# Inverse roots moved to ScalarE and VectorE in the attention part, scatters without an address check in the expert part

## What is computed

```python
q = q / jnp.linalg.norm(q, axis=-1, keepdims=True)      # k too, per head of 32
A = jnp.einsum('bnihd,bnjhd->bnij', Kb, K)              # chunks of 64 tokens
T = inverse of (I + tril(A, -1)); W = T @ Kb; U = T @ Vb
u_i = u0 - w_i * Sd[:, None]; o = q_i * Sd[:, None] + A_i[:, :, None, None] * u_i
o = o * jax.lax.rsqrt(jnp.mean(o * o, axis=-1, keepdims=True) + EPS) * g
x = _layernorm(x + o @ Wo)                              # (x - m) / sqrt(v + eps)
# router: sigmoid, 4 of 8 groups, the best 8 of 64 experts, weights normed
x = _layernorm(x + shared(x) + sum of 8 chosen expert MLPs)
```

## Time and profile before

| | us |
|---|---|
| median of 3 runs | 1161.55 |
| span of the profiled execution, first to last instruction | 868.7 |
| median less that span | 292.9 |
| TensorE matmuls busy in the span | 698.5 (80%) |
| GpSimd busy | 548.9 (63%) |
| VectorE busy | 489.8 (56%) |
| ScalarE busy | 322.0 (37%) |
| mean granted TensorE clock | 0.881 |

### The profile page before, as it was taken

The page is one execution under the profiler, slowest core; times in us unless marked ns, Lnnn a source line. Parts: engine busy times, 40 slices in busy tenths (PEclk is TensorE's granted clock), DMA queues, the critical chain, the costliest instruction groups (busy, mean ns, idle before and its releaser), DMA issues.

```text
span 868.7 us, 17014 instructions
## 1 busy us (share of the span) xinstructions
PE 698.5 (80%) x4968; PEld 606.5 (70%) x4968; DVE 489.8 (56%) x1679; ACT 322.0 (37%) x867; POOL 548.9 (63%) x558
## 2 busy tenths in 40 slices
PE   5689797979888786767799998999897888961395
PEld 3567676767676666644587898988797887960385
DVE  2437878787777777755756663444334433430275
ACT  2224233333424242313043564664545536420032
POOL 0000277777777777676777777777777777777241
PEclk9898989897979796959579998999989989895599
DMA  8202041414141413111354444444434434311695
GB/s 199 77 1 89 15 140 59 144 62 142 59 142 60 137 52 107 51 61 47 98 149 123 118 122 126 117 108 130 115 102 127 110 100 115 104 41 51 263 408 215
DMA packets 89949, 97.47 MB, mean 112 GB/s; under 512 B 21836, under 2 KB 73780, under 8 KB 89859
## 3 DMA queue, kind: packets, MB, share of 16 engines
q1 hardware_dynamic: 67043, 58.45, 23.5%
q0 software_dynamic: 20992, 36.74, 12.5%
q10 hardware_dynamic: 1824, 1.19, 0.5%
HBM read 55.02 MB, written 42.34 MB: 112 GB/s over the span
## 4 chain that ended last, share of the span: by engine, by line
PE 38%; DVE 22%; issue 15%; POOL 12%; DMA 7%; SPq 2%; ACT 2%; POOLq 0%; ACTq 0%; DVEq 0%
POOL y_dram L463 12%; DMA y_dram<-arena 4%; PE fa L1215 3%; PE fc L1140 3%; PE pb L1165 3%; PE pa L1165 2%; PE fb L1140 2%; PE ba L1145 2%; DMA arena<-y_dram 2%; DVE arena L720 2%; PE fa L1145 2%; PE bb L1140 1%; PE bb L1361 1%; PE ba L1361 1%; PE fb L1382 1%
## 5 line engine op out<-in xcount | busy, mean ns | idle before, releaser
L463 POOL DMA_INDIRECT y_dram<-arena x272 | 266.4, 979 | 83.4 <-issue 73.8
L444 POOL DMA_INDIRECT rows_dram<-rows x256 | 256.9, 1004 | 97.6 <-issue 76.4
L435 POOL TENSOR_TENSOR rstd<-var_eps,minus_half 128x2 f32<-128x2 f32 (+1 forms) x24 | 25.3, 1055 | 132.6 <-DVE var_eps L662 132.6
L618 ACT ACTIVATE arena<-weights 128x176 f32 x384 | 99.0, 337 | 13.8 <-DVE arena L1025 13.2
L1079 DVE TENSOR_TENSOR arena<-bb,arena 128x512 f32<-128x512 f32 x34 | 23.5, 691 | 75.5 <-DMA y_dram<-arena 70.9
L1140 PE MATMUL fb<-arena 128*128 128x128 f32 x384 | 53.7, 284 | 14.6 <-DVE arena L720 14.0
L1140 PEld LDWEIGHTS fb<-arena 128*128 128x128 f32 x384 | 48.8, 195 | 20.9 <-DVE arena L720 13.5
L1079 DVE TENSOR_TENSOR arena<-ba,arena 128x512 f32<-128x512 f32 x34 | 23.5, 690 | 67.1 <-DMA y_dram<-arena 63.3
L1140 PEld LDWEIGHTS fc<-arena 128*128 128x128 f32 x384 | 50.0, 197 | 15.2 <-ACT arena L522 7.7
L607 ACT ACTIVATE arena<-fb 88x512 f32<-88x512 f32 x39 | 23.1, 592 | 99.3 <-PE fc L1382 89.2
L1361 PE MATMUL bb<-weights,arena 88*128 x336 | 47.9, 293 | 14.4 <-DVE arena L1113 13.8
(11 more groups left out here) (295 smaller groups left out, 1472.6 us busy)
## 6 DMA issues: line engine op xcount, KB each, us to landing
arena<-y_dram SPq DMA_DIRECT2D x16, 1024.0 KB, 12.1
arena<-rows_dram SPq DMA_DIRECT2D x192, 76.0 KB
weights<-experts SPq DMA_DIRECT2D x16, 608.0 KB
arena<-rows_dram SPq DMA_DIRECT2D x128, 38.0 KB
y_dram<-arena POOLq DMA_INDIRECT x272
rows_dram<-rows POOLq DMA_INDIRECT x256, 2.3
xc<-x_chan SPq DMA_DIRECT2D x8, 256.0 KB, 3.9
x_res<-x_tok SPq DMA_DIRECT2D x8, 256.0 KB, 3.0
```

Source lines behind the costliest of these rows:

```text
L435: pool.tensor_tensor(rstd[b % 2][:, 0:tiles], var_eps[b % 2][:, 0:tiles], minus_half[:, 0:tiles], ALU.pow).then_inc(S.rstd_done, 1)
L444: pool.indirect_dma_start(rows_dram, bass.IndirectOffsetOnAxis(ap=slot_of(a)[:, i, k:k + 1], axis=0), rows[:, NT * a + i, :], None).then_i ...
L463: pool.indirect_dma_start(y_dram, bass.IndirectOffsetOnAxis(ap=go_to[:, t:t + 1], axis=0), y_sb[q % YRING][:, i, :], None, bounds_check=B ...
L618: ins = act.activation(w_here[n % 2][:, (parts(q) * i + h) * 2 * I:(parts(q) * i + h + 1) * 2 * I], weights[:, bass.ds(at[i], 2 * I)], ACT ...
```

## The change

1. The inverse roots of the head norms and of the RMS norm: `Sqrt` on ScalarE (`hrt`, `rrt`, with scale and epsilon in the instruction) and `reciprocal` on VectorE (`hrn`, `rrn`), in place of 12 and 13 small VectorE instructions.
2. The layer norm of the first part: `Sqrt` on ScalarE (`std`), `reciprocal` on VectorE (`rstd`), in place of the added epsilon and GpSimd's power. The end part keeps the power.
3. The transposed inverse at level 0: a transpose on TensorE (`invt0`) and a copy on ScalarE (`cpt0`), in place of an identity written by ScalarE (`eyet`) and a masked copy on VectorE.
4. `cs` waits for `p2` only before its second half.
5. New slots for all steps of the first part and for the shared steps; the scatters of the first part stand alone in GpSimd's queue, one sequence after the other, without `SPREAD`.
6. The scatters of the second part have no bound check. `y_dram` gets 2048 rows in front, and unused rows are written there, each to a row of its own within four quads.

```diff
-NOWHERE = 1 << 20
+RING, YRING, W_RING = 4, 4, 6
+SINK = 4 * YRING * P
...
-AT = dict(proj0a=14, proj0b=23, silu0=43, sq0=50, sum0=52, proj1a=45, proj1b=47, silu1=62, sq1=80, sum1=88, proj2a=61,
...
-          sc=372, r0=358, r1=359, r2=360, r3=371, r4=373, r5=374, r6=375, r7=377, rank=380, r8=382, key0=385, key1=387,
-          key2=391)
-SPREAD = (401, 405, 406, 407, 411, 412, 422, 424, 426, 427, 438, 442, 447, 456, 457, 461, 470, 474, 475, 476, 479, 494,
...
+AT = dict(proj0a=10, proj0b=63.4, proj1a=72.63, proj1b=81.59, proj2a=83.6, silu0=84.07, silu1=94.35, sq0=95.07,
...
+          r5=376.43, r6=376.6, r7=376.88, sc=379.11, r8=380.99, key0=386.62, key1=387.17, key2=387.63, rank=392.19)
...
-SHARED = ({"t": 289.01, "c": 275.01, "g0": 289.02, "s0": 295.01, "m0": 309.01, "g1": 289.03, "s1": 295.02, "m1": 309.02, "d": 319.01, "a": 322.01},
...
+SHARED = ({"t": 241.81, "c": 243.4, "g0": 280.81, "s0": 263.29, "m0": 285.9, "g1": 285.45, "s1": 269.79, "m1": 299.31,
+           "d": 317.75, "a": 318.13},
...
-        y_dram = nc.dram_tensor("y_dram", [B * L * PLACES, D], F32, kind="Internal").ap()
+        y_dram = nc.dram_tensor("y_dram", [SINK + B * L * PLACES, D], F32, kind="Internal").ap()
...
-            def inverse_std(b, tiles=NT):
-                pool.wait_ge(S.ve_done, b + 1)
-                pool.tensor_tensor(rstd[b % 2][:, 0:tiles], var_eps[b % 2][:, 0:tiles], minus_half[:, 0:tiles],
+            def inverse_std(u):
+                pool.wait_ge(S.ve_done, u + 1)
+                pool.tensor_tensor(rstd[u % 2][:, 0:2], var_eps[u % 2][:, 0:2], minus_half[:, 0:2],
                                    ALU.pow).then_inc(S.rstd_done, 1)
...
-            for _, a, n in sorted([(a * CYCLE + AT["rstd"], a, -1) for a in range(B)]
-                                  + [(a * CYCLE + at, a, n) for a in range(B) for n, at in enumerate(SPREAD)]):
-                if n < 0:
-                    inverse_std(a)
-                else:
+            for a in range(B):
+                for n in range(NT * TOPK):
                     scatter(a, n)
...
                     pool.indirect_dma_start(y_dram, bass.IndirectOffsetOnAxis(ap=go_to[:, t:t + 1], axis=0),
-                                            y_sb[q % YRING][:, i, :], None, bounds_check=B * L * PLACES - 1,
-                                            oob_is_err=False).then_inc(ys[q % YRING], 16)
+                                            y_sb[q % YRING][:, i, :], None).then_inc(ys[q % YRING], 16)
             for u in range(PAIRS):
                 if u >= 2:
                     pool.wait_ge(S.ln2_done, u - 1)
-                inverse_std(B + u, 2)
+                inverse_std(u)
...
+                if op == "hrt":
+                    act.wait_ge(S.ss_done, NT * (a + 1))
+                    if a >= 1:
+                        act.wait_ge(S.hrn_done, a)
+                    act.activation(head_rt[:, :], head_ss[:, :], ACT.Sqrt).then_inc(S.hrt_done, 1)
...
-                if op == "eyet":
...
+                for k in range(LEVELS - 1):
+                    if op == f"cpt{k}":
+                        act.wait_ge(S.invt_mm, (LEVELS - 1) * a + k + 1)
+                        if k == 0 and a >= 2:
+                            act.wait_ge(S.tr_mm, a - 1)
+                        act.activation(inv_t[n], fa[:, :], ACT.Copy).then_inc(S.invt_done, 1)
...
+                if op == "rrt":
+                    act.wait_ge(S.t_done, a + 1)
+                    if a >= 1:
+                        act.wait_ge(S.rrn_done, a)
+                    act.activation(rms_rt[:, :], rms_ss[:, :], ACT.Sqrt, bias=rms_eps[:, 0:1],
+                                   scale=1.0 / HD).then_inc(S.rrt_done, 1)
+                if op == "std":
+                    act.wait_ge(S.mv_done, a + 1)
+                    if a >= 2:
+                        act.wait_ge(S.rs_done, a - 1)
+                    act.activation(std[n][:, :], mean_var[n][:, :, 1], ACT.Sqrt, bias=ln_eps[:, 0:1]).then_inc(S.std_done, 1)
...
-            def seed(x, half, y, sem, at):
-                dve.tensor_scalar(half, x, 0.5, None, ALU.mult)
-                dve.tensor_scalar(y.bitcast(U32), x.bitcast(U32), 1, None, ALU.logical_shift_right).then_inc(sem, 1)
-                dve.wait_ge(sem, at + 1)
-                dve.tensor_scalar(y.bitcast(U32), y.bitcast(U32), -1.0, float(0x5f3759df), ALU.mult, ALU.add).then_inc(sem, 1)
-            def newton(half, y, step, sem, at):
-                dve.wait_ge(sem, at)
-                dve.tensor_tensor(step, y, y, ALU.mult).then_inc(sem, 1)
-                dve.wait_ge(sem, at + 1)
-                dve.tensor_tensor(step, step, half, ALU.mult).then_inc(sem, 1)
-                dve.wait_ge(sem, at + 2)
-                dve.scalar_tensor_tensor(out=y, in0=step, scalar=1.5, in1=y, op0=ALU.subtract, op1=ALU.mult).then_inc(sem, 1)
...
-                dve.wait_ge(S.mv_done, b + 1)
-                dve.tensor_scalar(var_eps[n][:, 0:tiles], mean_var[n][:, 0:tiles, 1], LN_EPS, None, ALU.add).then_inc(S.ve_done, 1)
...
-                dve.wait_ge(S.rstd_done, b + 1)
...
-                if op == "seed":
-                    dve.wait_ge(S.ss_done, NT * (a + 1))
+                if op == "hrn":
+                    dve.wait_ge(S.hrt_done, a + 1)
                     if a >= 1:
                         dve.wait_ge(S.qk_done, a)
-                    seed(head_ss[:, :], half_ss[:, :], head_rn[:, :], S.rn_done, 11 * a)
-                for m in range(3):
-                    if op == f"newt{m}":
-                        newton(half_ss[:, :], head_rn[:, :], step_ss[:, :], S.rn_done, 11 * a + 2 + 3 * m)
+                    dve.reciprocal(head_rn[:, :], head_rt[:, :]).then_inc(S.hrn_done, 1)
...
-                    dve.scalar_tensor_tensor(out=qk, in0=qk, scalar=-1.0, in1=by_head, op0=ALU.mult,
+                    dve.scalar_tensor_tensor(out=qk, in0=qk, scalar=1.0, in1=by_head, op0=ALU.mult,
...
-                if op == "cpt0":
-                    dve.wait_ge(S.nat_done, a + 1)
-                    dve.wait_ge(S.eye_t_set, a + 1)
-                    dve.copy_predicated(by_tile(inv_t[n]), mask_of(0, 1), by_tile(fa[:, :])).then_inc(S.invt_done, 1)
...
-                    dve.wait_ge(S.t_done, a + 1)
-                    dve.tensor_scalar(rms_ss[:, :], rms_ss[:, :], 1.0 / HD, RMS_EPS, ALU.mult,
-                                      ALU.add).then_inc(S.orms_done, 1)
-                    dve.wait_ge(S.orms_done, a + 1)
+                if op == "rrn":
+                    dve.wait_ge(S.rrt_done, a + 1)
                     if a >= 1:
                         dve.wait_ge(S.on_done, a)
-                    seed(rms_ss[:, :], half_rms[:, :], rms_r[:, :], S.orr_done, 11 * a)
-                for m in range(3):
-                    if op == f"rnewt{m}":
-                        newton(half_rms[:, :], rms_r[:, :], step_rms[:, :], S.orr_done, 11 * a + 2 + 3 * m)
+                    dve.reciprocal(rms_r[:, :], rms_rt[:, :]).then_inc(S.rrn_done, 1)
...
-                    dve.scalar_tensor_tensor(out=heads(o_sb), in0=heads(o_sb), scalar=-1.0,
+                    dve.wait_ge(S.rrn_done, a + 1)
+                    dve.scalar_tensor_tensor(out=heads(o_sb), in0=heads(o_sb), scalar=1.0,
...
-                if op == "shift":
+                if op == "rstd":
+                    dve.wait_ge(S.std_done, a + 1)
                     if a >= 2:
                         dve.wait_ge(S.x1_done, a - 1)
+                    dve.reciprocal(rstd[n][:, :], std[n][:, :]).then_inc(S.rs_done, 1)
+                if op == "shift":
+                    dve.wait_ge(S.rs_done, a + 1)
                     shifted(a)
...
-                    dve.tensor_scalar(go_to[:, 4 * q:4 * q + 4], w_at[q % W_RING][:, :, 1], float(NOWHERE), None, ALU.add).then_inc(S.go_done, 1)
+                    dve.tensor_tensor(go_to[:, 4 * q:4 * q + 4], w_at[q % W_RING][:, :, 1],
+                                      const[:, K_SINK + 4 * (q % YRING):K_SINK + 4 * (q % YRING) + 4], ALU.max).then_inc(S.go_done, 1)
...
+                    dve.wait_ge(S.mv_done, B + u + 1)
+                    dve.tensor_scalar(var_eps[u % 2][:, 0:2], mean_var[u % 2][:, 0:2, 1], LN_EPS, None, ALU.add).then_inc(S.ve_done, 1)
...
+                if op == "invt0":
+                    pe.wait_ge(S.nat_done, a + 1)
+                    pe.wait_ge(S.inv_done, LEVELS * a + 1)
+                    turned(fa, lambda i: blk(inv, i)).then_inc(S.invt_mm, 1)
...
-                    pe.wait_ge(S.p1_done, a + 1)
-                    pe.wait_ge(S.p2_done, a + 1)
                     pe.wait_ge(S.invt_done, (LEVELS - 1) * (a + 1))
                     for m, p in enumerate((p1, p2)):
+                        pe.wait_ge((S.p1_done, S.p2_done)[m], a + 1)
                         for i in range(NT):
                             mm = pe.matmul(fa[:, m * NC + 2 * i:m * NC + 2 * i + 2], p[:, i, :],
```

(13 more changed lines are left out.)

51 lines of the change are left out of this document (26 added, 25 removed).

## The result

The changed kernel takes 1216.24 us (median of 4 runs, 1214.87 to 1219.74), the kernel before 1160.39 us beside it (4 runs, 1156.73 to 1168.6). The ratio is 1.0461, 95% interval 1.0414 to 1.0508: slower, where I had forecast 1145.

The account below looks back on a forecast made before the run. It took a hand-over chain to bound the first part and GpSimd the second, gated by TensorE at quad 8. 868.7 - 11.8 (earlier quad 8) - 4.6 (scatters) = 852.3, plus 292.9 outside the span: 1145 us, range 1133 to 1160.

Parts of the forecast that it names:

- (c): Layer norm of the first part: variance to shift takes about 0.5 us in place of 1.43, -0.9 per cycle.
- (a): RMS norm: from sum to scaling 0.55 us in place of 2.86, -2.3 per cycle.
- (f): New slots, projections mostly beside router and levels 2 to 5: no row; from losing the norms' gains to gaining nothing more.
- (b): Head norm: its seed and Newton step no longer stand ahead of cs, -1.3 us per cycle.
- (g): Start: first head norm about 1.3 us in place of 2.55; first cs at 59.2 in place of 61.52.
- (d): Table loads, three per cycle: ahead of hrt hidden, ahead of tanh +0.2 us, ahead of SiLU 0, at most 1.28.
- (h): Between the parts: more TensorE work behind the ranks, +7 us (bounds +3 and +11); first quad 11.8 us earlier.
- (i): GpSimd's first part ends 20.8 us earlier, at 438.8; then it waits some 9 us for TensorE before quad 8.
- (j): Second part's scatters without bound check: 960 in place of 979 ns, 4.6 us won (bounds 0 and 5).
- Rival 2: A table switch blocks ScalarE twice as long, 2.57 us; cycle 45.1, slower at 1169.7 us; chance 0.12.
- Rival 1: Between the parts, TensorE's tail is no longer than before and GpSimd is the gate: -26, 1135.5 us; chance 0.18.
- Rival 3: The first part's cycle hardly moves, 44.2 us, as bunched projections on TensorE eat VectorE's savings: 1157 us; chance 0.20.

Follow-up runs that it names:

- the slow profile of before: The kernel before, unchanged, profiled again in a group where all runs were slow: 1191.27 us, span 1189.5.
- the version with the break: The changed kernel with GpSimd waiting before scatter 17 of each first-part burst for the next sequence's moments: 1149.36, then 1145.92 us (0.9862, 0.9827 of before), slow.
- the two parts: Roots and slots alone, and unchecked scatters with sink rows alone, each put into the kernel before: 841.93 and 864.28 us, before 871.36.
- the version with the roots alone: The change's roots and slots, second part's scatters checked as in the kernel before: ratio to before 0.9683 quick, 1.0421 slow.
- a paced first part: The changed kernel with one small useless GpSimd pow after every second scatter of the first part: 1044.48 us, 0.8994 of before, slow.

## Why the prediction was wrong, step by step

**The step that failed** is the last of the sum: "With the 292.9 us between its span and the median of the runs: 1145." I took the gap for something around the span, the same for both kernels. It lies inside: less than 2 us lie around the span of any run here, and the slow profile of before has its 320 us more than the quick one (1189.5 for 869.1) in both parts and between them (137, 161 and 22), with TensorE, VectorE and ScalarE held while GpSimd scatters. The profile I read had no such hold. Every stall I priced came from a condition that the timed runs were not in.

**The term that was missing**: GpSimd's `pow` between scatters 17 and 18 broke each burst. I counted it in (c) as a part of the chain from variance to `shift`, and put what the wait ahead of it did for the other engines at nothing, without a reason. In the profile that I read, the break is short:

```profile
126.94 1.08 POOL L435 TENSOR_TENSOR rstd<-var_eps,minus_half 128x4 f32<-128x4 f32 x1 [1.97 <-DVE var_eps L662]
```

The first six of these waits there are 1.1 to 2.9 us long, where in the slow profile above the first is 8.21 and the second 11.82. In the slow condition the break was worth 70 us, more than all that the roots bring: 1219.5 without and 1145.9 with a break, where before takes 1164.9. Once it is back, roots, slots and unchecked scatters together gain 14 to 19 us there. My 16 was thus near, but of the version with the break, and near by luck: in the quick condition, where my rows were taken, the two parts gave 29.4 and 7.1 us, over twice the sum that I had made for it.

**(a) to (f), the cycle**, in the quick condition, where the rows that I used belong, in the version with the roots alone. The RMS norm in its chain:

```profile
109.33 0.70 DVE rms_ss L769
110.05 0.32 ACT rms_rt L545
110.39 0.26 DVE rms_r L775
110.68 0.70 DVE arena L778
```

0.65 us from sum to scaling (0.55 said; 2.86 before). (b) and (g): the first `cs` comes at 58.9, for 61.8 in the kernel before in the same condition, 2.9 us earlier (2.3 said). (c) 115.28 to 116.40 in the same chain, 1.1 from variance to the ACTIVATE that uses it, where I had 0.5 to `shift`. (d) Its loads, in ScalarE's timeline:

```profile
118.29 0.60 ACT L567 ACTIVATE arena<-ba 128x512 f32<-128x512 f32 x1 [0.75 <-PE ba L1142]
118.90 1.28 ACT L572 ACT_TABLE_LOAD   x1
120.20 0.38 ACT L572 ACTIVATE arena<-br 128x256 f32<-128x256 f32 x1
...
137.12 0.42 ACT L493 ACTIVATE arena<-arena 128x256 f32<-128x256 f32 x1
137.56 1.28 ACT L499 ACT_TABLE_LOAD   x1
138.85 0.23 ACT L499 ACTIVATE head_rt<-head_ss 128x32 f32<-128x32 f32 x1
```

The load ahead of `tanh` ends 0.14 behind the logits (120.04): +0.2 holds. The one ahead of `hrt`, which I had counted as hidden, stands on the chain that ended last. The one ahead of SiLU (120.60) isn't on that chain. (f) is where I was too careful, and the term that was most mis-sized: `cs` comes at 58.9 (59.2 said) and then every 40.6 us up to sequence 4 (40.7 up to sequence 7, 343.5), where I said 42.5:

```profile
L1215 PEld LDWEIGHTS fa<-const,arena x16: 186/192/193, 98.8 to 100.5; 128*128 128x128 f32 x16
L1215 PEld LDWEIGHTS fa<-const,arena x16: 186/192/193, 221.2 to 222.9; 128*128 128x128 f32 x16
```

(221.2 - 58.9) / 4. So the cycle is 4.2 us shorter than the 44.86 of before, not 2.36. My own stations gave 41.6; the 0.9 of gaps on top never came. In the slow condition the first cycle, nearly all of it ahead of the first scatter, was 40.1 (60.8 to 100.9 in the changed kernel), and from then on the scatters ruled.

**(h), (i)** The last instruction of the last `cs` starts 33.9 us earlier (345.2 for 379.1, against the kernel before in the same condition) where I had 18.8, and the last scatter 29.8 (778.8 for 808.6), so between them 4.1 us are given back, not 7. GpSimd waits in small pieces, 1.7 and 1.9 us at most, not 9 ahead of quad 8.

**(j)** Right in the quick condition: 958 ns for 978, and -7.1 us for -4.6. In the slow one nothing that shows: 1218.49 against 1219.52.

**The rivals.** Rival 2 had the sign and the wrong cause. A load costs its 1.28 us and no more: it starts 0.02 us behind a ScalarE that was busy till then and ends 0.01 ahead of the next ACTIVATE. The Trainium skill (ScalarE: Activation LUTs, "What ACT_TABLE_LOAD costs") adds a drain of about 1380 ns to each switch; the trace doesn't agree. Rival 1 is nearest to the quick condition (-26 for the -29.4 and -7.1 of the parts; the changed kernel itself was never met in that condition). Rival 3 had the cycle at 44.2, and it is 40.7; rival 4 is out, as the same rows of 128 words take 958 ns without the check and 978 with it. None of them named the scatters' effect on the other engines.

**What stays open**: why the engines' results are late. In the first part the hold comes with scatters at 1.27 us apiece, it begins some 10 us into a burst, it ends with the burst, and it is there in the slow condition alone; the packets, the bytes and the duration of a scatter are those of the quick one. The condition isn't a property of one chip: the chips numbered 0 and 10 were each met quick in one group of runs and slow in another. Whether it sits in the chip or in the recording, which all timed runs share, no run here tells. Nor is there a version that was measured to beat the kernel before in both conditions: the roots alone do in the quick one (0.968), the change with one break in the slow one (0.983, interval 0.976 to 0.989), and that with a paced first part by far (0.899, slow only). What a break costs in the quick condition was never measured.

## What to carry to other kernels

When a span and the runs' times lie a quarter apart, the profile is of another condition than the runs: settle that first, since no stall read from it is one of those timed. Before an instruction is taken from between DMA-issuing ones, ask what its wait did for the pace of the others: here one wait that looked like dead time was worth 70 us. And where a profile names no cause for a wait, follow a single result from the instruction that wrote it to the one that reads it: here that showed which hand-over was late. Time a change in every condition that the machine shows, because the sign can turn: 0.968 and 1.042 for the very same kernel.

## What was not expected of the hardware

- A scatter burst of 32 at 1.27 us apiece brings TensorE from 5.0 to between 1.2 and 1.9 matmuls per us after 10 us in the slow condition. At 1.55 us apiece it goes on at 5.5.
- In such a burst a result of TensorE is read 9.0 us after its matmuls' recorded end, where in a quick profile the same one is read after 0.03 us.
- 4.2 us of useless `pow` on GpSimd per sequence made the kernel 92 us quicker there (1221.45 to 1129.29, runs from 1119.32 to 1149.79), 16 single ones of 0.57 us per sequence 177 us (1044.48).
- A small `Sqrt` on ScalarE that reads its epsilon from a tile takes 0.30 us (128x4) and 0.31 (128x16), a reciprocal of 128x16 on VectorE 0.25, both more than the small rows that I had for them (0.21 and 0.18).
- Three table loads per sequence, each 1.28 us, with 0.02 us to the instruction on either side.
